# A graph convolution in fp32 on one core: scaled x in any tile slot, second loads all at the end, POOL summing some tiles

## The reference

```python
A = adj + jnp.eye(adj.shape[0], dtype=adj.dtype)
deg = jnp.sum(A, axis=1)
d_isqrt = jax.lax.rsqrt(deg)
A_hat = A * d_isqrt[:, None] * d_isqrt[None, :]
h = jnp.matmul(A_hat, x)
x = _layernorm(x + jax.nn.elu(jnp.matmul(h, w)), axis=-1)
```

## Time and profile before

| | us |
|---|---|
| median of 3 runs | 1122.17 |
| lowest, highest | 1121.51, 1123.5 |
| profiled execution | 1121.2 |
| its span, first to last instruction | 1119.4 |
| PE busy in the span | 942.1 |
| DVE busy | 857.2 |
| ACT busy | 720.1 |
| POOL busy | 78.9 |

### The profile page before, as it was taken

One profiled execution on the slowest core, in us unless ns is written; L12 is line 12 of the kernel. 1 busy time (PEld: TensorE's weight loads), 2 busy tenths in 40 slices (PEclk: granted clock), 3 DMA queues, 4 the chain that ended last, 5 costly groups with the idle time before them and its releaser, 6 DMA issues.

```text
span 1119.4 us, 38626 instructions
## 1 busy us (share of the span) xinstructions
PE 942.1 (84%) x17408; PEld 856.9 (77%) x17408; DVE 857.2 (77%) x870; ACT 720.1 (64%) x1865; POOL 78.9 (7%) x87
## 2 busy tenths in 40 slices
PE   0089399599496798899899999999999999999992
PEld 0089388488386688889898999989889899867682
DVE  0677676765756696978899999997879987889746
ACT  6899898978977799979996857454352210133134
POOL 0000000000000000000000000000000000023124
PEclk9999789799799899999999999999999999999996
DMA  9999999989999699989999999897889868989312
GB/s 379 384 396 405 383 355 402 375 320 400 347 387 388 230 388 378 386 318 384 395 356 388 369 327 315 300 316 252 287 284 334 306 201 296 299 261 324 105 40 76
DMA packets 173764, 359.07 MB, mean 321 GB/s; under 512 B 6048, under 2 KB 30752, under 8 KB 166432
## 3 DMA queue, kind: packets, MB, share of 16 engines
q1 hardware_dynamic: 156704, 348.21, 85.9%
q10 hardware_dynamic: 16896, 8.39, 2.6%
HBM read 352.39 MB, written 4.19 MB: 319 GB/s over the span
## 4 chain that ended last, share of the span: by engine, by line
PE 67%; issue 10%; DMA 8%; DVE 6%; SPq 3%; ACT 3%; POOL 3%; POOLq 0%; DVEq 0%
PE p_set L632 67%; DMA tile<-in_adj 8%; SPq L488 3%; DVE tile L651 3%; ACT tile L537 2%; DVE xs L670 1%; POOL tile L516 1%; POOL rstd L526 1%; ACT xs L545 1%; DVE hT L682 1%; SPq L481 0%; POOL var_eps L522 0%; DVE tile L709 0%; DVE xn L663 0%; DVE stats L697 0%
## 5 line engine op out<-in xcount | busy, mean ns | idle before, releaser
L632 PE MATMUL p_set<-tile,xs 32*128 32x256 f32 (+3 forms) x17280 | 924.0, 371 | 154.1 <-ACT xs L545 91.9
L632 PEld LDWEIGHTS p_set<-tile,xs 32*128 32x128 f32 x17280 | 840.9, 190 | 234.3 <-issue 165.5
L537 ACT ACTIVATE tile<-tile 128x512 f32<-128x512 f32 (+2 forms) x828 | 594.3, 719 | 200.8 <-DMA tile<-in_adj 192.6
L651 DVE STREAM_TRANSPOSE tile<-tile 128x2048 f32<-128x2048 f32 x256 | 579.9, 2291 | 77.2 <-ACT tile L537 73.8
L682 DVE TENSOR_TENSOR hT<-p_set,hT 128x512 f32<-128x512 f32 (+1 forms) x202 | 151.2, 780 | 131.7 <-PE p_set L632 130.9
L537 ACT ACTIVATION_READ_ACCUMULATOR tile<-tile 128x1 f32 x828 | 154.5, 187 | 0.0
L545 ACT ACTIVATE xs<-xn 32x512 f32<-32x512 f32 x96 | 60.1, 626 | 73.5 <-PE p_set L632 55.0
L569 ACT ACTIVATE tile<-p_set,d 128x128 f32<-128x128 f32 x64 | 18.2, 366 | 104.5 <-PE p_set L618 104.5
L505 POOL TENSOR_TENSOR tile<-tile,ident 128x512 f32<-128x512 f32 x16 | 20.4, 1272 | 783.8 <-ACT tile L537 783.8
L670 DVE COPY xs<-xn 32x512 f32<-32x512 f32 x160 | 67.8, 424 | 4.2 <-PE p_set L632 1.9
L516 POOL TENSOR_TENSOR tile<-tile 128x512 f32<-128x512 f32 x16 | 20.4, 1276 | 127.6 <-DVE tile L689 127.5
(11 more groups left out here) (14 smaller groups left out, 27.2 us busy)
## 6 DMA issues: line engine op xcount, KB each, us to landing
tile<-in_adj SPq DMA_DIRECT2D x325, 1024.0 KB, 11.2
xn<-in_x SPq DMA_DIRECT2D x16, 256.0 KB, 11.7
tile<-in_x ACTq DMA_DIRECT2D x16, 256.0 KB, 3.1
out_rows<-tile ACTq DMA_DIRECT2D x16, 256.0 KB, 3.4
tile<-in_adj SPq DMA_DIRECT2D x4, 768.0 KB, 10.2
w_sb<-in_w SPq DMA_DIRECT2D x1, 64.0 KB, 2.0
```

The lines of the kernel that those rows point to most:

```text
L537: ins = nc.scalar.activation(view[:, g], view[:, g], ACT.Copy, accum_out=to[:, g:g + 1])
L632: ins = nc.tensor.matmul(to, xs[quadrant(q), t % XRING, j], turned[quadrant(q), j], start=j == 0, stop=j == GROUPS - 1)
L651: nc.vector.transpose(tiles[slot_of[k]], tiles[slot_of[k]]).then_inc(tile_turned, 1)
```

## The change

- The ring `xs` goes. Scaled x of a band ("home", 2048 numbers in a partition) lies in any tile slot; slots are 22 in place of 19. A home takes a slot when x is asked for and gives it back when its band's first-load products are done, for bands below STAY = 13 also if second loads are still to come.
- `KEEP` is 14 for strips below 9 and 5 from there.
- The next strip may not be more than AHEAD = 2 past the oldest band with first loads undone.
- All second loads come after all firsts, in groups of rows (`row_groups`): rows in falling order, two in a group, three in the first. A group is one PSUM job that sums over its bands, with one add at its end. Bands without a home are asked for again; ACT makes all 16 copies ("recopy").
- A product of a single first tile is made only if no other tile of its band is on the way.
- POOL may sum a far tile by nine halving additions ("halve") if ACT is busy when the tile lands.
- PE waits for x's copies by piece s, and its matmuls go piece by piece.
- Normalising moves from DVE to ACT, with a small `shift` on DVE.

The diff, cut to its core:

```diff
--- before.py
+++ after.py
@@ -10,25 +10,28 @@
...
-SLOTS = 19
+SLOTS = 22
 LATE = 3
-KEEP = 12
-XRING = 3
+KEEP = (14, 9, 5)
+AHEAD = 2
...
 XN = 2
...
 EPS = 1e-5
+COPIES = {"dve": [(s, q) for s in (0, 1) for q in range(Q)] + [(2, 0), (2, 1)], "act": [(2, 2), (2, 3)] + [(3, q) for q in range(Q)]}
+HALVES = [(1, 2.4), (1, 1.35), (2, 1.3), (5, 1.3)]
...
 def kept_units():
 
     alive, kept = [0] * BANDS, set()
     for t, r in sorted(((t, r) for t in range(BANDS) for r in range(t + 1)), key=lambda v: (v[0], -v[1])):
-        if all(alive[m] < KEEP for m in range(r, t + 1)):
+        if all(alive[m] < (KEEP[0] if m < KEEP[1] else KEEP[2]) for m in range(r, t + 1)):
             kept.add((t, r))
             for m in range(r, t + 1):
                 alive[m] += 1
...
+def row_groups(agains):
+
+    rows = sorted({u for _, _, u in agains}, reverse=True)
+    sizes = [3] + [2] * len(rows) if len(rows) % 2 else [2] * len(rows)
+    groups = []
+    while rows:
+        n = sizes.pop(0)
+        groups.append([v for v in agains if v[2] in rows[:n]])
+        rows = rows[n:]
+    return groups
...
+    def ask_x(t):
+
+        nonlocal dma
+        if not free or len(homes) >= XN and copied.get(len(homes) - XN) != 2:
+            return False
+        home_of[t] = len(homes)
+        homes.append((t, take_slot(("home", len(homes)))))
+        order["sp"].append(("x", home_of[t]))
+        dma = max(dma, now + 1.0) + XLOAD
+        if t in known:
+            offer("dve", 5, "scale", home_of[t], 0.7)
+        return True
+
+    def drop_home(t):
+        release(homes[home_of.pop(t)][1])
...
+        if row_todo and at_row > oldest + AHEAD:
+            pick_row = False
+        else:
+            pick_row = bool(row_todo) and not (row_todo[0][0] == "first" and len(free) < 2)
+        if firsts and (backlog < FEED or not pick_row):
+            return firsts.pop(0)
+        if pick_row:
             return row_todo.pop(0)
-        if pick and len(slots) > 1:
-            (firsts if pick[0] == "first" else agains).remove(pick)
-            return pick
+        if rows_done and not firsts and not row_todo:
+            return next_again()
         return None
+
+    def next_again():
+
+        nonlocal group_at, group_todo
+        if len(late) < LATE:
+            return None
+        if not group_todo:
+            if group_at + 1 == len(last_groups):
+                return None
+            bands = sorted({v[1] for v in last_groups[group_at + 1]}, reverse=True)
+            for t in bands:
+                if t not in home_of and not ask_x(t):
+                    return None
+            group_at += 1
+            group_todo = sorted(last_groups[group_at], key=lambda v: (v[1] if group_at == 0 else -v[1], v[2]))
+            group_open.append([set(last_groups[group_at]), sorted({v[2] for v in last_groups[group_at]})])
+            if not free:
+                return None
+        return group_todo.pop(0)
...
+            if sum(1 for h, (t, _) in enumerate(homes) if t == homes[arg][0] and h < arg):
+                offer("act", 4, "recopy", arg, 0.64 * len(ALL_COPIES))
+            else:
+                offer("dve", 0, "copies", arg, 0.43 * len(COPIES["dve"]))
+                offer("act", 0, "copies", arg, 0.64 * len(COPIES["act"]))
...
+                if loads[k][0] == "first":
+                    first_left[t] -= 1
+                    backlog -= 1
+                else:
+                    again_left[t] -= 1
+            if not first_left[t] and (not again_left[t] or t < STAY and not rows_done):
+                drop_home(t)
+            if last:
+                offer("dve", 1, "add", job, 0.15 + 0.55 * len(jobs[job][1]))
...
+        if free_set() is not None:
+            groups = [even_slots([k for k in tiles_ready if loads[k][0] == "first" and loads[k][1] == t]) for t in range(BANDS)]
+            groups = [g for g in groups if len(g) > 1 or g and not any(loads[k][:2] == ("first", loads[g[0]][1]) for k in coming)]
+            if groups:
+                ks = max(groups, key=lambda g: (min(len(g), 2), -loads[g[0]][1]))
+                for k in ks:
+                    tiles_ready.remove(k)
+                job = open_job([loads[k][2] for k in ks], {loads[k][2]: 1 for k in ks})
+                parts.append((job, home_of[loads[ks[0]][1]], ks, True, True))
+                return len(parts) - 1
...
+            for t in sorted({loads[k][1] for k in here}, reverse=True):
+                ks = sorted((k for k in here if loads[k][1] == t), key=lambda k: loads[k][2])
+                want = [v for v in left if v[1] == t]
+                if len(ks) < len(want):
+                    continue
+                at = [slot_of[k] for k in ks]
+                gaps = {b - a for a, b in zip(at, at[1:])}
+                if len(gaps) > 1 or any(abs(g) > 15 for g in gaps):
+                    ks = ks[:1]
...
+                offer("pool", 3, "halve", (arg, 0), HALVES[0][1])
             else:
-                offer("act", 5, "sum", arg, sum_took(load))
+                offer("act", 5, "sum", arg, sum_took(loads[arg]))
         elif what == "stored":
             counts["stored"] += 1
         else:
...
+                    k, step = arg
+                    _, r, k0, nk, x0, wide = loads[k]
+                    if not step:
+                        pool.wait_ge(loaded[slot_of[k]], arrived[k])
+                    done = sum(many for many, _ in HALVES[:step])
+                    for n in range(done, done + HALVES[step][0]):
+                        if n:
+                            pool.wait_ge(pool_halved, HALVINGS * (halve_nth[k] - 1) + n)
+                        w = wide >> (n + 1)
+                        view = shaped(k)
+                        if n < HALVINGS:
+                            nc.gpsimd.tensor_tensor(view[:, :, 0:w], view[:, :, 0:w], view[:, :, w:2 * w], ALU.add).then_inc(pool_halved, 1)
+                        else:
+                            pieces = sums[:, BLOCKS * r + k0:BLOCKS * r + k0 + nk, x0 // BAND:x0 // BAND + w]
+                            nc.gpsimd.tensor_tensor(pieces, view[:, :, 0:w], view[:, :, w:2 * w], ALU.add).then_inc(pool_summed, 1)
+                elif kind == "diagonal":
                     k = arg
                     pool.wait_ge(act_summed, sum_nth[k])
...
-            def copies(t):
-
-                act.wait_ge(x_scaled, scale_nth[t])
-                wait_xs_free(act, t)
-                for s, q in COPIES["act"]:
-                    ins = nc.scalar.activation(xs_part(t, q, s), xn[quadrant(s), t % XN], ACT.Copy)
-                ins.then_inc(copied_by["act"], 1)
+            def copies(h, pairs):
+
+                act.wait_ge(x_scaled, scale_nth[h])
+                wait_vacant(act, ("home", h))
+                for s, q in pairs:
+                    nc.scalar.activation(xs_part(h, q, s), xn[quadrant(s), h % XN], ACT.Copy).then_inc(copied_by["act"], 1)
 
...
+            def normalise(n):
+
+                act.wait_ge(shift_ready, n + 1)
+                for b in range(BLOCKS):
+                    ins = nc.scalar.activation(pos[:, n % RING, b], pos[:, n % RING, b], ACT.Identity,
+                                               bias=shift[:, n % RING, b:b + 1], scale=rstd[:, n % RING, b:b + 1])
+                ins.then_inc(normed, 1)
...
-                    t, ks = products[arg]
-                    for copies in ("dve", "act"):
-                        pe.wait_ge(copied_by[copies], copied[copies][t])
-                    pe.wait_ge(tile_turned, max(turn_nth[k] for k in ks))
...
+                job, h, ks, first, last = parts[arg]
+                bank, rows, _ = jobs[job]
+                if first:
+                    wait_set_free(pe, ("job", job))
+                pe.wait_ge(tile_turned, max(turn_nth[k] for k in ks))
...
+                for s in range(Q):
+                    if h in recopied:
+                        pe.wait_ge(copied_by["act"], copied["act"][h] + Q * (s + 1))
+                    else:
+                        for engine in ("dve", "act"):
+                            some = [i for i, c in enumerate(COPIES[engine]) if c[0] == s]
+                            if some:
+                                pe.wait_ge(copied_by[engine], copied[engine][h] + max(some) + 1)
+                    for b in range(BLOCKS):
+                        j = Q * b + s
                         for q in range(Q):
-                            to = p[:, q, 0:128 * len(at)]
-                            to = to.rearrange("f (g i) -> f g i" if len(at) == 1 else "f (n g i) -> f n g i", g=BLOCKS, i=32)
-                            ins = nc.tensor.matmul(to, xs[quadrant(q), t % XRING, j], turned[quadrant(q), j],
-                                                   start=j == 0, stop=j == GROUPS - 1)
-                    ins.then_inc(product_out, 1)
+                            chunk = tile[quadrant(q), at[0], 32 * j:32 * j + 32]
```

(62 more changed lines are left out.)

340 lines of the change are left out of this document (196 added, 144 removed).

## The result

The changed kernel takes 1090.34 us (median of 4, 1088.72 to 1091.17) against 1122.69 in the same comparison: ratio 0.9711, 95% interval 0.9694 to 0.9728. The forecast was 1104 and its range 1080 to 1138, so the gain was 32 us where 18 were expected.

What follows compares the result with a forecast made beforehand. Loads set the pace first, TensorE afterwards. First part 756, between the parts 8, tail 318 and close 20 make 1102, plus 1.8 around the span: 1104 us, range 1080 to 1138.

Steps and rivals of the forecast that it cites:

- End of the first part, 756: TensorE finishes the 173 first-load tiles at 748 to 771 us, taken as 756.
- early pace: Loads up to band 3 took 2.73 us a unit; rival that this pace holds: 1083 us, chance 0.24.
- Singles: "this only fills idle time, thus 0": Fewer one-tile products, 10 to 15 in the first part: worth 0 while loads bound, about 2 us each later.
- Between the parts, 8: TensorE's loss before second loads arrive, 5 us, plus 3 us for later homes.
- The tail, 318: Second-load products: 39 pairs 273 us, 5 singles 25, 14 closing products and wait 20, sum 318.
- The close, 20: From the last pass over tiles to the end: 20 us, where it was 26 before.
- Waits by piece, 2.5 once: PE starting after x's first four copies gains 2.5 us once, inside the 756, as band starts don't add up.
- POOL, taken 0, 10 to 25 tiles of 7.1 us: POOL sums 10 to 25 of 83 far tiles, 7.1 us each; gain 0 to 10 us, taken 0.
- Normalising, at most 1: Moving normalising from DVE to ACT changes the closing chain by at most 1 us either way.
- The starvation rival: In the tail TensorE runs dry waiting for homes: 40 to 60 us in place of 8, 1136 to 1156, chance 0.16.
- The lock rival: POOL and DVE block each other at band starts or POOL's sums come late: 18 to 24 us lost, chance 0.06.

Runs made afterwards that it cites:

- The early splits: Changed kernel with 15 products of two tiles in bands 1 to 4 (every second one) made as two passes of one tile each: 1145.27 us.

## Why the prediction was right, and where its size was off

*End of the first part, 756.* It came at 753.8, but by two errors that met. Band 7's copies began at 499.6, not at 520 to 543: the pace was 2.62 us a unit, faster than the "early pace" of 2.73. In return TensorE had only 102 tiles behind it at band 7's first pass, by the plan's order, not 110; from 560 on it was itself the bound (191 of 194 us busy until 754).

*Singles: "this only fills idle time, thus 0".* This step failed. An early single costs 3.7/2 = 1.8 us in the total, like a late one, by way of late slots and slower loads. There were 7 in the first part by the plan's order, where 10 to 15 were expected. Fewer singles are part of why the loads ran at 388 GB/s: with the rule undone they ran at 372. By the page's sums cheaper passes are 30 of the 32 us, but the rule alone gives nothing in the kernel before. Which part of the change makes it pay stays open, and the parts are not additive: the rule undone loses 51 us, more late kept tiles 35 and two slots fewer 49, of a gain of 32.

*Between the parts, 8.* It was under 3. The hole in the queue came, 51 us long, and 7 tiles and what was left of the firsts covered it.

*The tail, 318.* Exactly 39 pairs and 5 singles, by the plan; 311.5 us from 756.6 to 1068.1. A pair takes 55.5/8 = 6.94 in a stream.

*The close, 20.* 19.6. *Sum:* about 2 for the first part, 5 between the parts and 7 in the tail make the 14 us between forecast and result.

*Waits by piece, 2.5 once.* Worth 8.4. That band starts don't add up was wrong here. The early splits say the same: the waits at later starts took up none of their cost.

*POOL, taken 0, 10 to 25 tiles of 7.1 us.* 15 tiles, 7.1 us each; worth nothing that two pairs of runs show.

*Normalising, at most 1.* About 3, not clear of the spread.

*The starvation rival* (0.16) did not happen, but the kernel is near it: recopies twice as long cost 44 us. What the slowed recopies then met was not empty slots or late x but ACT's order.

*The lock rival:* the Trainium skill's rule ("SBUF — State Buffer", "Who interferes with whom") agrees with these traces: a copy of 0.42 us lasts up to 2.46 beside POOL's 1024-column addition of 2.4. The holds are a few us at single band starts, and the two pairs of runs with and without POOL's halvings show no loss.

## What to carry to other kernels

A pass over weights that serves one tile can cost its full extra time even where TensorE waits for loads, if those loads wait for its slots: price it in that stage too. Test a scheduling rule in both kernels; here it was worth 51 us in one and 0 in the other, probably because it needs room to wait in. When comparing waits of two traces, take the start out of both: a trace can book it to another line. Before putting a long batch on an engine that also frees PSUM, look at what stands behind it in that queue.

## What the runs showed of the hardware that was not expected

DVE's copies and POOL's additions: ten copies of 4.2 us lasted 8.0 beside one chain of halvings, and a scale of 0.65 us up to 2.14 (up to 1.76 without the halvings). The chain itself was as long as its columns foretold: 7.1 us.
